# Attention scores with keys on partitions, maxima in a first pass, and an unnormalised float32 product

## The reference, cut to what matters

```
x = x + xattn(layernorm(x), ctx)          # x (2, 256, 256), ctx (2, 512, 64)
x = x + moe(layernorm(x))                 # 32 experts, top 4, and a shared one

q_big = rope(einsum('bshk,hkq->bshq', (hidden_q @ Wq.T), w_kc_q))     # 16 heads
q_r   = einsum('bshq,hqr->bhsr', q_big, W_qr);  kv_r = rope(ctx)
k_r   = einsum('bld,hdr->bhlr', kv_r, W_kr)
scores = einsum('bhsr,bhlr->bhsl', q_r, k_r)                          # 256 x 512 each
attn   = softmax(scores, axis=-1)
ctx_c  = einsum('bhsl,bld->bhsd', attn, kv_r)
out    = (ctx_c with w_kc_kv, then Wo)
```

## Time and profile before

| | |
|---|---|
| median of 3 runs | 361.36 us (359.24 to 363.11) |
| the profiled execution | 359.29 us, span 357.5 us |
| PE / DVE / ACT / POOL busy | 278.3 / 230.8 / 172.1 / 139.1 us |
| attention loop on the profile's clock | about 32 to 224 us |

### The profile page before, as it was taken

One profiled execution on the slowest core, in us unless ns is written; L12 is line 12 of the kernel. 1 busy time (PEld: TensorE's weight loads), 2 busy tenths in 40 slices (PEclk: granted clock), 3 DMA queues, 4 the chain that ended last, 5 costly groups with the idle time before them and its releaser, 6 DMA issues.

```text
span 357.5 us, 5400 instructions
## 1 busy us (share of the span) xinstructions
PE 278.3 (78%) x1670; PEld 200.1 (56%) x1670; DVE 230.8 (65%) x574; ACT 172.1 (48%) x402; POOL 139.1 (39%) x126
## 2 busy tenths in 40 slices
PE   3767779899898998989989899595379999994000
PEld 3544558766586765867758788454335555552000
DVE  4476844889897898978987687568604444443133
ACT  3434745866777786876865564520023333330000
POOL 0733903984029670196900000000364544400672
PEclk9989999999999999999999999859679999998555
DMA  7910033000420003300029937100134444412242
GB/s 255 400 55 0 3 91 146 0 0 0 131 107 3 1 2 105 116 2 0 2 63 360 402 147 265 59 0 1 34 100 125 143 134 140 140 62 75 75 137 81
DMA packets 17595, 35.41 MB, mean 99 GB/s; under 512 B 2848, under 2 KB 10272, under 8 KB 17568
## 3 DMA queue, kind: packets, MB, share of 16 engines
q1 hardware_dynamic: 15264, 28.77, 22.6%
q0 software_dynamic: 2304, 6.29, 6.0%
HBM read 29.81 MB, written 5.24 MB: 98 GB/s over the span
## 4 chain that ended last, share of the span: by engine, by line
PE 50%; DVE 19%; issue 7%; ACT 6%; POOL 4%; DMA 2%; POOLq 0%; another core or an unknown queue 0%; ACTq 0%; DVEq 0%
PE bank L557 8%; PE bank L508 6%; PE bank L493 5%; PE bank L573 4%; PE bank L465 4%; POOL ctT L1101 4%; DVE nmax L837 3%; PE bank L548 3%; PE bank L443 2%; DVE pT L850 2%; PE bank L485 2%; PE bank L484 2%; PE bank L390 2%; PE bank L392 2%; PE bank L391 2%
## 5 line engine op out<-in xcount | busy, mean ns | idle before, releaser
L1096 POOL DMA_INDIRECT rope<-xn_rows,idx x32 | 30.5, 954 | 102.0 <-DVE idx L1005 76.6
L303 POOL TENSOR_TENSOR rtmp<-abuf,rope 128x512 f32<-128x512 f32 x22 | 29.2, 1326 | 73.5 <-issue 58.1
L837 DVE TENSOR_REDUCE nmax<-bank 128x1 f32<-128x512 f32 x64 | 43.5, 682 | 15.0 <-PE bank L485 14.0
L704 ACT ACTIVATE prob<-bank,nmax 128x512 f32<-128x512 f32 x48 | 33.1, 689 | 30.1 <-DVE nmax L837 29.6
L850 DVE TENSOR_TENSOR pT<-bank,pT 128x512 fp32r<-128x512 f32 x64 | 43.5, 681 | 1.9 <-ACT pT L712 1.9
L712 ACT CAST pT<-bank 128x512 fp32r<-128x512 f32 x64 | 37.6, 590 | 6.7 <-PE bank L493 6.3
L508 PE MATMUL bank<-pT,kvs 128*128 128x256 f32 x256 | 38.2, 292 | 0.8 <-DVE pT L850 0.6
L557 PE MATMUL bank<-wall,nmat 128*64 (+1 forms) x256 | 35.8, 402 | 0.2 <-ACT nmat L756 0.2
L493 PE MATMUL bank<-ident,prob 128*128 128x128 f32 x192 | 29.5, 278 | 6.2 <-DVE pT L850 5.4
L1011 DVE TENSOR_TENSOR kv<-bank,kv 128x128 f32<-128x128 f32 x32 | 9.3, 292 | 38.1 <-issue 30.8
L508 PEld LDWEIGHTS bank<-pT,kvs 128*128 128x128 f32 x256 | 32.4, 189 | 2.3 <-issue 1.1
(11 more groups left out here) (172 smaller groups left out, 530.2 us busy)
## 6 DMA issues: line engine op xcount, KB each, us to landing
wall<-in_w_exp SPq DMA_DIRECT2D x32, 384.0 KB, 7.3
y_rows<-nmat SPq DMA_DIRECT2D x32, 128.0 KB, 1.7
wring<-in_w_attn SPq DMA_DIRECT2D x16, 224.0 KB, 3.9
wring<-in_w_attn SPq DMA_DIRECT2D x4, 640.0 KB, 7.8
wring<-in_w_attn SPq DMA_DIRECT2D x4, 512.0 KB, 6.8
rope<-in_rope_q SPq DMA_DIRECT2D x1, 768.0 KB, 6.8
x_sb<-in_x SPq DMA_DIRECT2D x1, 512.0 KB, 3.6
xn_rows<-xn SPq DMA_DIRECT2D x4, 128.0 KB, 1.8
```

Of the source, the lines that this page charges most:

```text
L704: act.activation(probs[t % 4], s_ps[t % 3][:, :], ACT.Exp, bias=nmax[:, t:t + 1], accum_out=psum_e[:, t:t + 1]).then_inc(s_exp, 1)
L837: dve.tensor_reduce(nmax[:, t:t + 1], s_ps[t % 3][:, :], AX.X, ALU.max, negate=True).then_inc(s_max, 1)
L1096: pool.indirect_dma_start(xg[:, u % XG, :], None, xn_dram, bass.IndirectOffsetOnAxis(idx[:, 1, u:u + 1], 0)) \
```

## The change

A tile is now 128 keys of one head pair and one batch entry against 2 x 256 queries; four tiles are a group `n` (16 groups). The keys are the weights and the queries stream, so exp's result has keys on partitions, as the product with the context needs it. The transposes, both halves of the probabilities and the row-wise normalisation are gone. In their place:

- `maxima`: a first pass per group, four products of 512 columns over 64 rows, from the high halves alone, only to find each query's maximum (`row_max`, now of these).
- `shift_T` and `shift_row`: the negated maxima are transposed (a product with 4 output rows) and written as four extra rows of `q2`, against rows of ones in `kdup`. The scores' second product so has 68 rows and subtracts the maximum.
- `exps` is a plain exp into `pT`; `attend` is two float32 products per tile (one per head, 64 output rows each).
- `key_add` sums `pT` over the four key blocks on DVE, `sums` multiplies by ones, and `ctx` divides at the end: a reciprocal of 128x256 and a multiply, once per group.
- ACT writes two more copies for each pair's q (`q2`). The ring of q has 2 places instead of 4, with `q2` beside it.
- `PLAN` is new, and it now places rope tiles on DVE too (x, y, z: tiles 0, 1, 2 of a pair): 8 of 24 instead of 2.

```diff
-ROPE_V = 1
+QR = 2
+SLOOK, ALAG, MAX_AHEAD, SHIFT_AHEAD, SUM_LAG, CTX_LAG = 2, 1, (7, 6), 5, 5, 6
...
-        s_ps = bank[2:5]
-        t_ps = bank[5:7]
-        pv_ps = bank[7]
+        s_ps = bank[2:4]
+        m_ps = bank[4:6]
+        pv_ps = bank[6:8]
...
-            {0: "-N0", 1: "-N1", 2: "M0 M1", 4: "A0 B0", 6: "G0 C0 M2", 7: "M3", 9: "A1 B1", 10: "R0 R1", 11: "R2 C1", 12: "G1", 14: "P0", 15: "P1 P2"},
+            {1: "M0 M1", 2: "-N1 A0 B0 C0 x0", 3: "G0 M2", 4: "M3", 6: "R0", 7: "A1 R1 R2 B1", 9: "C1", 10: "G1", 12: "P0", 14: "P1 N0", 15: "P2"},
...
+            def maxima(n, st):
+
+                p, b = divmod(n, 2)
+                pe.wait_ge(q_lo, p + 1)
...
+                if st == 0 and n >= 1:
+                    pe.wait_ge(sh_row, n)
+                if st == 1:
+                    pe.wait_ge(mx_done, 4 * n + 2)
+                for h in range(2):
+                    r = slice(h * R, (h + 1) * R)
+                    pe.matmul(m_ps[h][:, :], qsp[r, p % QR, h, b * S + st * P:b * S + (st + 1) * P],
+                              kdup[r, 0, b * L:(b + 1) * L], start=True, stop=True).then_inc(mx_mm, 1)
+
+            def shift_T(n):
+                pe.wait_ge(mx_done, 4 * n + 4)
+                pe.matmul(m_ps[0][R:R + 4, 0:P], nmax[:, 4 * n:4 * n + 4], ident[:, :], start=True, stop=True).then_inc(sh_T, 1)
+
             def scores(t):
...
-                q = qsp[:, (h // 2) % 4, h % 2, b * S + st * P:b * S + (st + 1) * P]
-                pe.matmul(s_ps[t % 3][:, :], q, kdup[:, 0, b * L:(b + 1) * L], start=True, stop=False)
-                pe.matmul(s_ps[t % 3][:, :], q, kdup[:, 1, b * L:(b + 1) * L], start=False, stop=True) \
-                  .then_inc(s_mm, 1)
...
+                pe.matmul(s_ps[t % 2][:, :], kdup[:, 0, keys], qsp[:, p % QR, :, b * S:(b + 1) * S], start=True, stop=False)
+                pe.matmul(s_ps[t % 2][:, :], kdup[0:R + 4, 1, keys], q2[0:R + 4, p % QR, :, b * S:(b + 1) * S],
+                          start=False, stop=True).then_inc(s_mm, 1)
+
+            def attend(t):
...
+                for h in range(2):
+                    pe.matmul(pv_ps[n % 2][h * DC:(h + 1) * DC, 0:S], kvr[:, b * LC + c, 0, :], pT[:, n % 2, c, h * S:(h + 1) * S],
+                              start=(c == 0), stop=(c == LC - 1))
+
+            def sums(n):
+                pe.wait_ge(k_sum, n + 1)
+                for h in range(2):
+                    pe.matmul(pv_ps[n % 2][h * DC:(h + 1) * DC, S:2 * S], onec[:, :].to_broadcast([P, DC]),
+                              psum_k[:, n % 2, h * S:(h + 1) * S], start=True, stop=True).then_inc(pv_mm, 1)
...
+            for t in range(-MAX_AHEAD[0], TILES):
+                if 0 <= t + SLOOK < TILES:
+                    scores(t + SLOOK)
+                n, late = divmod(t + SHIFT_AHEAD, LC)
+                if late == 0 and 0 <= n < GRPS:
+                    shift_T(n)
+                for st in range(2):
+                    n, late = divmod(t + MAX_AHEAD[st], LC)
+                    if late == 0 and n < GRPS:
+                        maxima(n, st)
                 for s in steps(t):
                     step(*s)
+                if t >= ALAG:
+                    attend(t - ALAG)
...
+                    for h in range(2):
+                        last = act.copy(q2[0:R, p % QR, h, :], work[u % 2][h * R:(h + 1) * R, :])
+                    last.then_inc(wk_out, 1)
...
-                act.activation(probs[t % 4], s_ps[t % 3][:, :], ACT.Exp, bias=nmax[:, t:t + 1],
-                               accum_out=psum_e[:, t:t + 1]).then_inc(s_exp, 1)
+                act.activation(pT[:, n % 2, c, :], s_ps[t % 2][:, :], ACT.Exp).then_inc(s_exp, 1)
...
+            def key_add(n, c):
...
+                    dve.tensor_tensor(a, a, pT[:, n % 2, c, :], ALU.add).then_inc(k_add if c == 2 else k_sum, 1)
+
+            def ctx(n):
+                p, b = divmod(n, 2)
+                dve.wait_ge(pv_mm, 2 * n + 2)
+                dve.reciprocal(ctmp[:, n % 2, :], pv_ps[n % 2][:, S:2 * S]).then_inc(c_inv, 1)
+                dve.wait_ge(c_inv, n + 1)
+                dve.tensor_tensor(ctT[:, p, b * S:(b + 1) * S], pv_ps[n % 2][:, 0:S], ctmp[:, n % 2, :], ALU.mult).then_inc(c_sum, 1)
```

More of the change, by code:

```diff
@@ L451, in step @@
                         for dc in range(ND):
[L452 removed]
+                            mm = pe.transpose(m_ps[dc][:, tt * P:(tt + 1) * P], xn[:, tt, dc * P:(dc + 1) * P], ident[:, :])
                     mm.then_inc(xT_mm, 1)
@@ L497, in attend @@
-            def attend(hb):
-                b = hb % 2
-                pe.wait_ge(t_lo, 2 * hb + 2)
-                if hb == 0:
-                    pe.wait_ge(kv_split, 2)
-                if hb >= TILES // 2 - 2:
-                    pe.wait_ge(s_exp, TILES - 1)
-                elif hb >= 1:
-                    pe.wait_ge(c_sum, hb)
-                for n in range(2 * LC):
-                    lc, hl = n // 2, n % 2
-                    mm = pe.matmul(pv_of(hb), kvs[:, b * LC + lc, :], pT[:, hl, hb % 2, lc, :],
-                                   start=(n == 0), stop=(n == 2 * LC - 1))
-                mm.then_inc(pv_mm, 1)
+                    pe.wait_ge(k_ones, 1)
@@ L520, in _ @@
                 for s in steps(t):
                     step(*s)
-                transposes(t)
-                if t % 2 == 1 and t >= 3:
-                    attend((t - 3) // 2)
-            attend(TILES // 2 - 1)
+                if t >= ALAG:
+                    attend(t - ALAG)
+                n, late = divmod(t - SUM_LAG, LC)
+                if late == 0 and n >= 0:
+                    sums(n)
+            for t in range(TILES - ALAG, TILES):
+                attend(t)
+            for n in range((TILES - 1 - SUM_LAG) // LC + 1, GRPS):
+                sums(n)
@@ L864, in _ @@
-            inverse(0)
-            normalise(0)
-            for t in range(TILES):
-                if t + 1 < TILES:
-                    inverse(t + 1)
-                if t + LOOK < TILES:
-                    row_max(t + LOOK)
-                if t + 1 < TILES:
-                    normalise(t + 1)
-                if t >= 1:
-                    prob_lo(t - 1)
-                if t % 2 == 0 and t >= 4:
-                    ctx_sum((t - 4) // 2)
+            for t in range(-MAX_AHEAD[0], TILES):
+                n, late = divmod(t + SHIFT_AHEAD, LC)
+                if late == 0 and 0 <= n < GRPS:
+                    shift_row(n)
+                for st in range(2):
+                    n, late = divmod(t + MAX_AHEAD[st], LC)
+                    if late == 0 and n < GRPS:
+                        row_max(4 * n + 2 * st)
+                        row_max(4 * n + 2 * st + 1)
@@ L877, in _ @@
                 for s in steps(t):
                     step(*s)
-            prob_lo(TILES - 1)
-            ctx_sum(TILES // 2 - 2)
-            ctx_sum(TILES // 2 - 1)
+                if t % LC >= 1 and t > 0:
+                    key_add(*divmod(t, LC))
+                n, late = divmod(t - CTX_LAG, LC)
+                if late == 0 and n >= 0:
+                    ctx(n)
+            for n in range((TILES - 1 - CTX_LAG) // LC + 1, GRPS):
+                ctx(n)
             def x1(tt):
@@ L1082, in ropes @@
                 for k in range(NQT):
-                    if p < ROPE_V and k != 1:
+                    if (p, k) in BY_DVE:
                         continue
-                    pool.wait_ge(wk_out, use(g, "BBC"[k], j) + 1)
+                    pool.wait_ge(wk_out, max(use(g, kk, j) for kk in ("AB", "AB", "C")[k]) + 1)
                     rope_tile(pool, link, g, j, k, 2).then_inc(rope_p, 1)
```

214 lines of the change are left out of this document (91 added, 123 removed), and 6 rows, old and new, of the table PLAN.

## The result

The change makes the kernel slower: 389.34 us (384.77 to 392.86) against 361.28 us, ratio 1.0741 [1.068, 1.0801]. The forecast had 367 us and a range up to 380. The direction was right, the size was far off. The profiled execution took 386.11 us, 26.8 more than that of before (359.29).

A forecast was written before the change was run, and what follows sets the result against it. The prediction took PE to bound the attention loop, with DVE just under it. 14 - 5 - 2 = +7 on the profiled 359.3 us gave 366.3, stated as 367 us, with a range from 350 to 380.

The forecast's parts named there:

- PE's +14: Attention loop: PE needs 1.66 us a tile, 0.22 more than before, which makes +14 us for 64 tiles.
- a change of form and back: PE in the loop: leaving and re-entering the 64-row product form between scores and `attend` costs 0.28 us in every tile.
- Waits: -5: Loop: maxima running ahead and a shorter chain take back 5 us of PE's idle 16.3, between 0 and -10.
- the sum for DVE: Loop, 16 tiles: DVE needs 43.1 us where it had 39.2, staying just under PE's 45.4.
- The rope price: DVE in the loop: a rope operation or `key_add` costs 0.9 us, from 0.68 with POOL idle and 1.22 beside POOL.
- The second rival: Loop: DVE becomes the bound at 48.3 us for 16 tiles, PE waits on top, 376 us in all; chance 0.14.
- Start: -2: Start: DVE taking a rope tile from POOL outweighs later low half and scores; net -2 us, between +3 and -5.
- Tail and rest: 0: Behind the loop: new tail about as long as the old 4.8 us, routing and experts unchanged; 0 us.
- Reciprocal: DVE, once per group: the reciprocal of 256 elements takes 2.2 us by a slope of 8 ns an element.
- the first rival: Loop: PE's new products are cheap, at most 1.30 us a tile, DVE becomes the bound, 350 us; chance 0.28.

The follow-up runs named there:

- e3: Changed kernel with the loop's six later rope tiles back on POOL, only the first pair's two kept on DVE; 1.0262 of the kernel before.
- e4: Changed kernel with four unread float32 products added on PE ahead of `maxima` at four tiles, under the waits; 1.0517 of the kernel before.
- e15: Changed kernel with DVE's rope tiles kept, but POOL's from the second head group on replaced by copies of 8 elements; 1.0232 of the kernel before.
- e8: Kernel before with eight rope tiles on DVE instead of two, nothing else changed; 1.0426 of the kernel before.
- e7: e3 with DVE taking q's low halves after ACT's first two copies instead of all four; 1.0124 of the kernel before.
- e13: e7 with `attend` issued for two tiles in a row at even tiles, the sums left where they were; 1.0024 of the kernel before.
- e14: e13 with the `attend` pairs at odd tiles, so the sums stand directly behind a pair; 1.0015 of the kernel before.
- e16: e13 with a group's four `attend` tiles in a row and the sums directly behind them; 1.0157 of the kernel before.

## Why the prediction was wrong

- **PE's +14 was nearly right.** By rows, 1.24 + 0.22 for the maxima + 0.08 for `shift_T` + 0.12 for the sums, as set, is the 1.66 of the forecast, and a change of form and back has its 0.28. Over a whole head group it is 4.4 us for 16 tiles (e3), so 0.27 more a tile instead of 0.22, or +17.6 for 64. The loop's +13.6 agrees with +14 only because some steps moved ahead of its first scores; that match is luck.
- **"Waits: -5" is the step that failed**, with the sum for DVE on which it rests. It priced DVE as a sum over 16 tiles (43.1 us, under PE) and let what is under PE be covered. The sum itself was not bad: 40.5 and 45.8 us in the two middle groups of the changed kernel, which last 54.9 and 56.2. The order inside the stretch decided: 8 us of DVE work in a row ahead of the shift rows, for which PE waited 1.8 to 2.8 us at a time. PE's idle time in the loop is 205.0 - 189.4 = 15.6 against 18.1, so -2.4 instead of -5. In e3 it is 10.6, -7.4: there the step would have held. The 2.6 us are the small part; the larger one is what these waits set off.
- **What the waits set off was missing altogether**: three stretches of the loop at 1.2 GHz. Busy PE in the loop is 189.4 in the changed kernel and 177.4 in e3, which has the same products in it: 12 us. An estimate from the mean clocks agrees: 7% of 205.0 us against 1% of 181.8 is 12.5. e4 gave 9.8 back by filling the waits alone. This is the largest missed term; the forecast named the 1.2 GHz level only for the start, and put nothing for it in the loop.
- **The rope price.** I spread two kinds of time over DVE (0.68 alone, 1.22 beside POOL) and took 0.9. But 1.22 was misread: the group of the earlier trace rows has two operations, 0.68 with POOL idle and 1.755 beside POOL, and 1217 ns is their mean. The price of a meeting, 1.75, was in the trace of before. Now DVE and POOL work on tiles of the same pair at the same time, as from 110.6 us on, and the second operation of a tile meets POOL in six of eight tiles: means of 1.50 and 1.42, and the next `key_add` is held back too. The second rival had this in it, but priced as load (4 us a stretch, 376 us), not as delay. e15 shows that blocking and what follows are worth up to 19 us of the loop.
- **Start: -2 forecast, +8.3 up to the first scores.** 5.5 of the 8.3 are more busy PE, work that partly left the loop; 2.8 are idle time. I counted what DVE takes from POOL and not what it puts ahead of `row_max`: PE waited 3.48 us for that until 37.56. (A wait of 2.31 for q's low half, until 49.60, is in the loop.) In e3 the stretch is only 3.2 longer than before, so 5.1 of the 8.3 hang on the rope tile. What the start costs without the moved work was not measured.
- **Tail and rest: 0 forecast, -4.7 measured.** From the last scores to the end of the last output product it is 12.7 us before and 11.6 after, since less of the loop's work is left there. The other 3.6 lie in code that the change does not touch (131.1 and 127.5 us); no run shows why. The new kernels have 137 to 142 us behind their last scores.
- **Reciprocal**: 1.75 us, where 154 + 255 x 8 ns gave 2.2. The slope is (1750 - 154) / 255 = 6.3 ns for each further element.
Sum by the cuts of the table: 13.6 - 2.4 + 12 + 8.3 - 4.7 = 26.8. It closes because the cuts do; only the 12 stands for a cause by itself (e4), and the 13.6 and the 8.3 share the moved work. In the profiled executions 24.4 of the 26.8 us are gone with e3's plan, by the ratios 4.8 of 7.4%.

Two sums of the prediction do not come out. 366.3 plus the 2.1 that the median lies above the profiled execution is 368.4, not 367. And the terms of the first rival add up to about -15, not -13. Neither bears on the outcome.

The range ended at 380, because the second rival was thought of as one full engine. Two effects that both follow from one wait (later work, lower clock) were not added.

## What to carry to other kernels

An engine that is "under" the bound in the sum still works in an order: for each wait of the bound engine, add up what stands ahead of the awaited instruction on its own engine, at the times which those instructions have side by side with their neighbours. Work moved from one engine to another that shares its way to SBUF is not moved out of the way; e8 shows that +4.3% needs nothing else. A mean over two operations can hide both prices; read them one by one. And when PE loses microseconds while its busy share rises, read the granted clock before looking for more work.

## What the runs showed of the hardware

- Operations of 128x512 with two operands in SBUF take turns on DVE and POOL: on DVE 0.68 us alone and 1.64 to 1.78 us in a row beside POOL, whose own go from 1.26 to between 1.6 and 1.8. DVE operations that read a bank keep their times (1.74 for the division beside POOL, 1.75 with POOL silent in e15).
- The clock fell to 1.2 GHz behind single waits of 1.82, 2.50 and 2.84 us in a loop that was otherwise full; one of 2.17 us, until 91.42, had no fall behind it. Why that one didn't is open.
- Two products over 64 rows each, 512 columns, run side by side: 0.44 us for both with the change of form, where two of 128 rows take 0.24 each.
- A change between products of 128 weight columns and of 64 output rows, and back, costs 0.24 to 0.29 us of PE (e7, e13, e14, e16).
- One further element of a wide reciprocal costs 6.3 ns on DVE, against about 1 for the multiply from a bank (0.42 us for 256 elements) and the operations of 512 (0.68).
